# Turning the halves of q and k with transposing transfers instead of TensorE

## The reference

```python
x = layernorm(h); xn = layernorm(x) * norm_g + norm_b
q = split_heads(xn @ Wq); k, v = split_heads(x @ Wkv)
k, v = two learned null keys/values in front of each head's 2048
q = l2norm(q) * q_scale; k = l2norm(k) * k_scale
sim = 8 * q @ k.T - slope[head] * abs(key place - query place)
sim = where(causal, sim, -inf)
h = h + (softmax(sim) @ v) @ Wout
...
h = h + moe(layernorm(h)) + shared(layernorm(h))
```

## Time and profile before

| | us |
|---|---|
| median of 3 runs (2635.93 to 2639.04) | 2638.44 |
| the profiled execution | 2635.08 |
| its span | 2633.1 |
| PE busy | 2370.3 |
| DVE busy | 1816.8 |
| POOL busy | 1558.9 |
| ACT busy | 1419.1 |

### The profile page before, as it was taken

One profiled execution on the slowest core, in us unless ns is written; L12 is line 12 of the kernel. 1 busy time (PEld: TensorE's weight loads), 2 busy tenths in 40 slices (PEclk: granted clock), 3 DMA queues, 4 the chain that ended last, 5 costly groups with the idle time before them and its releaser, 6 DMA issues.

```text
span 2633.1 us, 47837 instructions
## 1 busy us (share of the span) xinstructions
PE 2370.3 (90%) x13353; PEld 1210.4 (46%) x13353; DVE 1816.8 (69%) x5108; ACT 1419.1 (54%) x3094; POOL 1558.9 (59%) x1645
## 2 busy tenths in 40 slices
PE   3789999999999999899999999999999998867897
PEld 2434444444444444444444444444444443456775
DVE  6668686767776788768686868686868686634445
ACT  2555656555555656565656565656565653323451
POOL 6365757575686666565757575757575755543424
PEclk9799999999999999899999999999999998868999
DMA  2000111111111011011111010101010021033544
GB/s 48 19 20 19 35 29 36 29 36 26 39 43 32 15 27 33 19 36 30 35 28 33 17 25 18 24 19 24 17 26 16 21 59 41 13 99 122 156 127 128
DMA packets 155691, 106.55 MB, mean 40 GB/s; under 512 B 63728, under 2 KB 139632, under 8 KB 155440
## 3 DMA queue, kind: packets, MB, share of 16 engines
q1 hardware_dynamic: 147760, 82.52, 12.4%
q0 software_dynamic: 7680, 20.98, 2.6%
HBM read 52.94 MB, written 33.29 MB: 33 GB/s over the span
## 4 chain that ended last, share of the span: by engine, by line
PE 68%; DVE 11%; POOL 9%; issue 7%; ACT 1%; DMA 1%; another core or an unknown queue 1%; SPq 1%; POOLq 0%; ACTq 0%; DVEq 0%
PE ps L1479 17%; PE ps L1463 9%; PE ps L1408 8%; PE ps L1464 7%; PE ps L1436 7%; POOL acc L794 5%; PE ps L1405 4%; DVE ps L1128 4%; PE ps L1499 4%; PE ps L1489 2%; PE ps L1560 2%; PE ps L1546 2%; PE ps L1420 2%; POOL rnorm L775 2%; DVE tqk L1102 1%
## 5 line engine op out<-in xcount | busy, mean ns | idle before, releaser
L794 POOL TENSOR_TENSOR acc<-acc,probs 128x512 f32<-128x512 f32 (+4 forms) x944 | 934.6, 990 | 326.7 <-ACT probs L924 240.6
L924 ACT ACTIVATE probs<-ps,btab 128x512 f32<-128x512 f32 (+4 forms) x1408 | 759.2, 587 | 649.9 <-PE ps L1464 367.0
L1128 DVE CUSTOM_DVE_ANT_0 ps<-ps,tab_l 128x512 f32<-128x512 f32 (+1 forms) x896 | 567.5, 674 | 324.5 <-PE ps L1436 321.9
L1479 PE MATMUL ps<-probs,arena 128*64 128x512 f32 (+4 forms) x2816 | 637.1, 528 | 0.2 <-DVE otf L1178 0.2
L1463 PE MATMUL ps<-arena 128*128 128x512 f16 (+4 forms) x1408 | 476.6, 340 | 0.3 <-DMA arena<-augs 0.3
L1464 PE MATMUL ps<-arena 128*128 128x512 f16 (+9 forms) x1408 | 471.6, 337 | 0.0
L1463 PEld LDWEIGHTS ps<-arena 128*128 128x128 f16 (+1 forms) x1408 | 135.5, 96 | 507.2 <-issue 336.6
L1436 PE MATMUL ps<-arena 64*128 64x512 f16 (+4 forms) x1408 | 245.0, 342 | 99.8 <-DVE mx L1128 95.9
L1408 PE MATMUL ps<-wqkv,xT 128*128 128x256 f32 (+1 forms) x1088 | 297.2, 398 | 0.1
L1128 DVE CUSTOM_DVE_ANT_0 ps<-ps,tab_r 128x258 f32<-128x258 f32 (+2 forms) x512 | 208.4, 448 | 97.2 <-PE ps L1436 94.0
L775 POOL TENSOR_TENSOR rnorm<-nsq,minus_half 128x8 f32<-128x8 f32 x144 | 226.0, 1570 | 12.0
(11 more groups left out here) (176 smaller groups left out, 3212.1 us busy)
## 6 DMA issues: line engine op xcount, KB each, us to landing
arena<-arena SPq DMA_DIRECT2D x512, 32.0 KB, 1.9
rl<-l_row SPq DMA_DIRECT2D x128, 128.0 KB
x_rows<-arena SPq DMA_DIRECT2D x78, 128.0 KB, 2.2
arena<-x_rows SPq DMA_DIRECT2D x78, 128.0 KB
y_rows<-arena SPq DMA_DIRECT2D x78, 128.0 KB
wqkv<-in_Wkv SPq DMA_DIRECT2D x32, 128.0 KB, 2.9
arena<-in_w SPq DMA_DIRECT2D x2, 2048.0 KB, 11.8
out<-h SPq DMA_DIRECT2D x8, 512.0 KB
```

The lines of the kernel that those rows point to most:

```text
L794: pool.tensor_tensor(a, probs[0:rows, (n - 2) % PB, 0:GW] if first else a, p, ALU.add).then_inc(sum_pool, 1)
L924: nc.scalar.activation(probs[0:rows, n % PB, 0:w], bank(S0 + n % 2)[0:rows, 0:w], ACT.Exp, bias=btab[0:rows, hh, z:z + 1]).then_inc(exp_do ...
L1128: nc.vector.tensor_tensor_reduce(bank(A0 + hd)[:, 0:w], bank(A0 + hd)[:, 0:w], tab, 1.0, NEG, ALU.add, ALU.max, mx[:, hd, it, c:c + 1]).th ...
L1479: mm(bank(O0 + o % 2)[DH * hd:DH * hd + DH, c0:GW], vt[t % 2][0:rows, jt, hd, :], probs[0:rows, n % PB, 0:GW - c0], start=(jt == 0), stop= ...
```

## The change

A half is turned by SP: `turn` becomes a kind of SP, which waits for `blk_ready` and issues four transposing DMA transfers of 128 x 256 fp16 from `blk` straight into `stk` (one of 16 rows for the ninth half). `keep` goes from ACT; what it did for the null keys is `null_k`. `copy_low` waits for the transfers. `turn` takes no shared PSUM bank any more. Each row of `stk` is padded from 2050 to 2064 columns. `aug` lies in unused columns of `blk`, 128 wide, cleared once, and is transposed whole. The stages have new places.

```diff
-    LAGS = [dict(square=0.3, ssq=1.05, inv=1.6, unit=2.0, high=3.3, low=4.1, turn=5.55),
-            dict(square=1.0, ssq=1.6, inv=2.8, unit=4.2, high=5.0, low=5.5, turn=7.0)]
+    LAGS = [dict(square=0.3, ssq=1.05, inv=1.6, unit=2.2, high=3.3, low=4.1, turn=5.55),
+            dict(square=0.6, ssq=1.6, inv=2.8, unit=4.2, high=5.0, low=5.8, turn=7.0)]
...
-                s1 = turn_of(s0 + lag["turn"])
+                s1 = s0 + lag["turn"]
                 at(s1, "turn", t, g)
-                at(s1 + 0.8, "keep", t, g)
-                at(s1 + 0.8 + 0.1, "copy_low", t, g)
-                halves[(t, g)] = s1 + 3.2
+                if g == 0:
+                    at(s1 + 3.6, "null_k", t)
+                at(s1 + 3.6, "copy_low", t, g)
+                halves[(t, g)] = s1 + 3.6 + 3.0
...
-                at(s0 + 0.5, "shift", t, ig)
+                at(s0 + 0.9, "shift", t, ig)
...
-                at(s1 + 1.5, "keep_shift", t, ig)
-                at(s1 + 1.5 + 0.1, "put_shift", t, ig)
-                shifts[(t, ig)] = s1 + 1.5 + 1.7
+                at(s1 + 1.2, "keep_shift", t, ig)
+                at(s1 + 1.2 + 0.1, "put_shift", t, ig)
+                shifts[(t, ig)] = s1 + 1.2 + 1.7
...
-            at(t0 + m - 0.9 * (m % 2) + 2.6, "sum_p", t, m)
-            at(t0 + (m | 1) + 2.95, "values", t, m)
+            at(t0 + m - 0.9 * (m % 2) + 2.9, "sum_p", t, m)
+            at(t0 + (m | 1) + 2.75, "values", t, m)
...
-            at(s0 + 3.15, "inv_l", t, ig)
-            at(s0 + 3.15 + 0.1, "spread_l", t, ig)
+            at(s0 + 3.65, "inv_l", t, ig)
+            at(s0 + 3.65 + 0.1, "spread_l", t, ig)
...
-    project(0, -24, 1.25)
+    project(0, -24, 1.32)
...
-        at(t0 + PAIR * t - 45.0 if t else -16, "tables", t)
+        at(t0 + PAIR * t - 43.0 if t else -16, "tables", t)
...
-        maxima(t, t0 + PAIR * t - 42.0, 1.92)
+        maxima(t, t0 + PAIR * t - 41.0, 1.92)
...
-    SHARED = ("proj", "sums", "turn_shift", "wout", "turn", "turn_x", "turn_y", "logits", "count", "null_turn")
+    SHARED = ("proj", "sums", "turn_shift", "wout", "turn_x", "turn_y", "logits", "count", "null_turn")
...
-        STK, LOW, VT = 2 * NK, 2 * NK, TK * 2 * DH
+        NS = N + 16
+        STK, LOW, VT = 2 * NS, 2 * NK, TK * 2 * DH
...
-        aug = sb("aug", [128, 2, 2, G], fp16)
+        aug = blk[:, :, 1024:1152]
...
+            def turn(t, g):
+                r = t % 2
+                sp.wait_ge(blk_ready, PG * t + g + 1)
+                need(sp, s_ready, PAIR * (t - 1))
+                if g < PG - 1:
+                    for z in range(2):
+                        for i in range(2):
+                            o, n = 512 * z + 256 * i, 256 * g + 128 * i
+                            sp.dma_start(stk[r][:, z, :, n:n + 128], blk[:, (PG * t + g) % 2, o:o + 256], transpose=True).then_inc(turned[g], 16)
+                else:
+                    sp.dma_start(stk[r][:, 1, :, N:NS], blk[0:16, (PG * t + g) % 2, 512:768], transpose=True).then_inc(turned[g], 16)
...
             def copy_low(t, g):
                 r = t % 2
-                sp.wait_ge(ta_done, PG * t + g + 1)
+                sp.wait_ge(turned[g], (64 if g < PG - 1 else 16) * (t + 1))
...
             def high(t, g):
                 act.wait_ge(qk_read, PG * t + g + 1)
-                need(act, tr_done, PG * t + g - 1)
+                k = PG * t + g - 2
+                if k >= 0:
+                    act.wait_ge(turned[k % PG], (64 if k % PG < PG - 1 else 16) * (k // PG + 1))
...
-            def keep(t, g):
...
+            def null_k(t):
+                p, r = t % NP, t % 2
+                act.wait_ge(turned[0], 64 * (t + 1))
+                nc.scalar.activation(stk[r][:, 1, :, 0:NN], null_ka[:, 2 * NN * p:2 * NN * (p + 1)].rearrange("p (a n) -> p a n", a=2),
+                                     ACT.Copy).then_inc(nk_in, 1)
...
-                tr(bank16(z)[0:2 * G, 0:128], aug[:, k % 2, :, :].rearrange("p a u -> p (a u)"), ident16[:, :]).then_inc(aug_tr, 1)
+                tr(bank16(z)[:, 0:128], aug[:, k % 2, :], ident16[:, :]).then_inc(aug_tr, 1)
```

More of the change, by code:

```diff
@@ L488, in lm_tower_kernel @@
         blk_ready = sem("blk_ready")
-        tr_done = sem("tr_done")
-        ta_done = sem("ta_done")
+        turned = [sem(f"turned{i}") for i in range(PG)]
         nk_in = sem("nk_in")
@@ L542, in lm_tower_kernel @@
         NPAR = 8
-        RELEASE = {"proj": p_read, "sums": l_read, "turn_shift": aug_kept, "wout": w_added, "turn": ta_done,
+        RELEASE = {"proj": p_read, "sums": l_read, "turn_shift": aug_kept, "wout": w_added,
                    "turn_x": xt_out, "turn_y": yt_out, "logits": lg_ready, "count": placed, "null_turn": null_ready}
@@ L678, in _ @@
                     spread_l(*which)
+                elif kind == "turn":
+                    turn(*which)
                 elif kind == "copy_low":
@@ L726, in constants @@
                 made(pool.memset(mask_b[:, :], 0.0))
+                made(pool.memset(aug[:, :, :], 0.0))
                 made(pool.affine_select(out=mask_a[:, :], in_=mask_a[:, :], compare_op=ALU.is_ge, fill=NEG, base=NN,
@@ L999, in _ @@
                     high(*which)
-                elif kind == "keep":
-                    keep(*which)
+                elif kind == "null_k":
+                    null_k(*which)
                 elif kind == "tables":
@@ L1139, in shift @@
                 need(dve, aug_tr, k - 1)
-                nc.vector.tensor_tensor(aug[:, k % 2, :, :], tab_g[:, :, its], rowmax[:, :, :], ALU.subtract).then_inc(aug_ready, 1)
+                nc.vector.tensor_tensor(aug[:, k % 2, 0:2 * G].rearrange("p (a u) -> p a u", a=2), tab_g[:, :, its], rowmax[:, :, :], ALU.subtract).then_inc(aug_ready, 1)
             def keep_shift(t, ig):
@@ L1409, in proj @@
                 last.then_inc(proj_done, 1)
[L1411 to L1425, removed]
             def scores_a(t, n):
@@ L1450, in scores @@
                     pe.wait_ge(aug_in[ig], 32 * (t + 1))
-                    pe.wait_ge(ta_done, PG * t + min(2 * ig + 3, PG))
+                    for g in range(min(2 * ig + 3, PG)):
+                        pe.wait_ge(turned[g], (64 if g < PG - 1 else 16) * (t + 1))
                     pe.wait_ge(nk_in, t + 1)
@@ L1606, in _ @@
                     proj(*which)
-                elif kind == "turn":
-                    turn(*which)
                 elif kind == "turn_x":
```

## The result

The changed kernel takes 2737.51 us, median of 4 runs (2732.56 to 2742.0); the kernel before, on the same chip, 2637.63 in 4 runs. The ratio is 1.0378, 95% interval 1.0361 to 1.0395: slower by 100 us. The forecast was 2596 us, with a range of 2550 to 2670. The first rival had 2740.

What follows compares the result with a forecast made beforehand. TensorE, busy 90% of the span, was taken as the bound except in a POOL stretch of some 15 us per pair. -49 us off the path and +7 for the first pair gave -42, so 2596 us, range 2550 to 2670.

Steps and rivals of the forecast that it cites:

- The first rival: On PE at scores_a: slow transposes land halves late, 2 us per issue, +105 us to 2740 us; chance 0.18.
- The relief of TensorE: On PE's chain: removing the transposes saves 44 us, and a wait for a shared bank 4.8 us more.
- take 1.0 us of issue each: On SP: each transposing transfer takes 1.0 us to issue, so a half takes 4 + 1.9, some 6 us.
- About as tight as now, so about as harmless: 0: Half's copies: 10.2 us against 10.0 us allowed by the plan, costing 0 if an issue is 1.0 us or less.
- A half's four issues (4 us) ahead of it are mostly swallowed: 0: On SP's queue, ahead of the row DVE's division needs: cost 0, at worst 1 to 2 us per pair.
- room: On SP: transposes and plain transfers fill 73 of 133 us per pair, and SP idles 687 us at L620 today.
- The first pair: Before the first attention: longer halves and copies behind SP's wait for the next half cost +7 us, from 0 to 15.
- New places: Moved stages on POOL and DVE, changing PE's waits for maxima: 0, with 30 us either way.
- PE's busy time: Sign in the changed profile: PE busy lower by 60 to 80 us.

Runs made afterwards that it cites:

- Experiment 4: Six of a half's eight TensorE transposes left out from the second pair on, no transfer added: 0.9906 in the kernel before, 1.0022 with the new places too.
- experiment 2: Changed kernel with eight transposing transfers per half instead of four: 1.2000; with blk and tqk by token tile, two 1.0135, four 1.0428, all against the kernel before.
- the tile layout: Changed kernel with columns of blk and tqk laid out by block of 128 tokens: four transfers 1.0428, two 1.0135 to the kernel before.

## Why the prediction was wrong

**The relief of TensorE** (-44 us of chain, -5 for a bank): right in kind, a little large. Experiment 4 gives about 35 us. The chain's share of a line was a fair measure for what taking it away is worth; the busy time, 79.8 us, would have been more than twice too much.

**"take 1.0 us of issue each"** and **"About as tight as now, so about as harmless: 0"**: the step that failed. Together they priced four more transfers per half in SP's queue at nothing. Measured are 1.25 to 1.27 us, and the landing takes 2.4 instead of 1.9. Four issues are 5.1 us; a half is 5.1 + 2.4 + 2.4 + 1.9 = 11.8 us (issues, landing, copies, landing) against the 10.0 of its allowance. PE then waits 28.7 us in ten pairs for the copies, where it waited 1.2. That the number of transfers is the cause, experiment 2 shows: 1.2000 and 1.0378 for eight and four, 1.0428 and 1.0135 for four and two in the other layout, with nearly the same packets. Rival 1 was said to decide only from 1.4 us per issue; the halves were late at 1.25 already.

**Rival 1's mechanism is what happened, though not at its price.** It had three waits of 4 us per pair, at `scores_a` alone, and 150 us of them as its sign; the runs show one wait per pair there of some 3 us, 45.6 in the whole stretch. The rest is spread over the landings, the exponentials, the division and longer matmuls. That 2740 was hit is in part luck: it rests on an issue of 2 us.

**"A half's four issues (4 us) ahead of it are mostly swallowed: 0"**: for the division, which it named, it was nearly right: PE waits 5.8 us for it in ten pairs, inside the "at worst 1 to 2 us per pair". What it left out is the other direction: the transposes, the copies and the shift row stand behind `spread_l`, which waits for its own row, and behind each other (661 to 678 us above). The sum counted SP's time (73 of 133 us, "room") where its order mattered, and the 687 us of idle time in the earlier trace rows said nothing of the places where SP was idle. With eight transfers (37.7 us) and with earlier projections (24.0) the division's row does become late.

**The first pair** (+7, at most 15): +17. The prediction sought it in the order of copy and wait; it was the load. Nine halves of 5.1 us of issue come at their densest there.

**New places** (0, 30 either way): not settled. They cost 1.1% with TensorE's turn, by waits that the changed kernel can't have, and with transfers no clean comparison was run.

**PE's busy time** was to fall by 60 to 80 us as a sign; it fell by 37. The unchanged matmuls last longer at the lower granted clock. No term of the sum allowed for that.

**The sum, as the runs have it.** The profiled executions differ by 104.6 us: 17.0 before the first attention, 73.5 in the pairs, 14.1 behind them. As the relief is worth some -35, the pairs have lost some 108. Going from four transfers to two in the tile layout gives back 57 of these (first to last scores 2283.0 and 2226.1 us), and 16 of the first 17. What makes up the other 50 or so is open: the two transfers that remain, the new places, and the lower granted clock (0.935 against 0.955 over the run), which comes together with more idle time of PE. Whether the clock would have stayed up without that was not tried; the longer matmuls are an estimated 24 us of the whole. The 14.1 behind the pairs are not shown to come from the transfers: on one other chip that stretch is 292.8, 293.6 and 295.0 us with two, four and eight of them.

The Trainium skill, "VectorE: DVE Perf Modes", section on the three transpose paths, gives 1309 ns for a 128x128 block through the crossbar. Here an issue takes 1.25 us, near that figure, and lands after 2.4, but for one, two or four such blocks at once. The prediction had multiplied the figure by eight blocks, and so taken, two transfers would cost the same as eight; the runs have 1.0135 and 1.2000, so the price goes by instruction. That this path is dearer than TensorE, for which the same table of the Trainium skill has 390 ns, held; the prediction weighed it too lightly.

None of the complete kernels tried here beats the one before. The nearest are TensorE's turn in the new places (1.0111) and two transfers (1.0135). Whether two transfers with a plan of their own would get below 1 was not found.

## What to carry to other kernels

Before moving work to a DMA queue, count instructions and not bytes, and write down what stands in that queue behind them at the densest 15 us, for the total of idle time hides it. Make each transposing transfer as large as the layout permits. If a product becomes ready later, follow it through every in-order queue that depends on it, and check that no stage now stands ahead of what it waits for. Before reading anything from an experiment on order, check in the plan that the order did change. Moving one stage mostly moved the wait. And compare PE's busy time for unchanged work too: what a change costs need not all be waiting.

## What the runs showed of the hardware

- A transposing transfer of fp16 between two places of SBUF takes SP 1.17 us to issue for 16 x 256, 1.23 for 128 x 128, 1.25 for 128 x 256, 1.26 for 128 x 512 (medians), against 0.6 for a plain one; it lands after 2.3 us (16 x 256), 2.4 or 2.5, against 1.9.
- With 528 of these transfers the change nearly doubled the run's DMA packets, 155,691 to 303,911; with 272 they are 295,719 and the kernel is at 1.0135.
- The same 12,297 matmuls keep PE busy 2333.0 us at a mean granted clock of 0.935 and 2442.2 at 0.879.
- 720 transposes of TensorE with 40.6 us of busy time are worth 25 us of execution.
